# A second set of open pages, one signal a pass, and evenly spaced indirect transfers in a routed mixture of experts with a recurrence

## What is computed

```python
xn = layernorm(x)
# attention part: a recurrence over tokens, with a gate
xn2 = layernorm(xn) * ln_w + ln_b
u = xn2 @ Ws.T + bs + xn2 @ Wi.T + bi              # 16 numbers a token
h = tanh(h @ A.T + u_t)                            # one token after another
s = (H @ Wo.T + bo) * sigmoid(xn2 @ Wg.T + bg) + xn
# feed-forward part: 16 experts, 4 chosen for each token, and a shared one
scores = sigmoid(xn @ gate_w.T)
idx = top_k(scores + gate_b, 4)
w = scores[idx] / sum(scores[idx]) * 2.5
y = sum over the 4: w_k * (silu(xn @ w1_k.T) * (xn @ w3_k.T)) @ w2_k.T
y = y + shared expert(xn)
out = x + s * silu(y)
```

## Time and profile before

| what | value |
|---|---|
| median of 3 runs | 443.7 us (442.36 to 444.87) |
| profiled execution, first to last instruction | 513.9 us |
| mean granted TensorE clock | 0.837 of full |
| TensorE, DVE, ACT, POOL busy | 339.1, 311.1, 251.0, 265.4 us |
| DMA | 109.27 MB, mean 213 GB/s |

### The profile page before, as it was taken

The page is one execution under the profiler, slowest core; times in us unless marked ns, Lnnn a source line. Parts: engine busy times, 40 slices in busy tenths (PEclk is TensorE's granted clock), DMA queues, the critical chain, the costliest instruction groups (busy, mean ns, idle before and its releaser), DMA issues.

```text
span 513.9 us, 10001 instructions
## 1 busy us (share of the span) xinstructions
PE 339.1 (66%) x3107; PEld 261.7 (51%) x3107; DVE 311.1 (61%) x977; ACT 251.0 (49%) x462; POOL 265.4 (52%) x278
## 2 busy tenths in 40 slices
PE   0365566849467786976799968797876968645210
PEld 0352443626355665755698846575654756433100
DVE  4899776676703545545643626786776555346745
ACT  1851666536434455443787746565664644422000
POOL 2005377766646566655600165766555554436773
PEclk9976698797876889888999989999997898676555
DMA  7998499425443566654779768899977777436653
GB/s 247 305 328 281 129 343 331 161 86 201 143 165 127 175 186 201 196 172 156 216 220 269 227 192 268 281 282 285 285 243 211 249 217 225 128 119 194 174 160 126
DMA packets 88675, 109.27 MB, mean 213 GB/s; under 512 B 9649, under 2 KB 78002, under 8 KB 88626
## 3 DMA queue, kind: packets, MB, share of 16 engines
q1 hardware_dynamic: 74656, 74.47, 45.7%
q0 software_dynamic: 12288, 33.57, 20.7%
q10 hardware_dynamic: 1682, 0.59, 0.4%
HBM read 55.91 MB, written 52.69 MB: 211 GB/s over the span
## 4 chain that ended last, share of the span: by engine, by line
PE 35%; another core or an unknown queue 12%; issue 10%; ACT 8%; DVE 6%; POOL 5%; DMA 1%; ACTq 1%; POOLq 0%; DVEq 0%
PE bank L850 13%; PE bank L872 8%; PE bank L656 6%; POOL xn_parts L638 5%; PE bank L863 3%; ACT xn_f L1851 3%; PE bank L898 2%; ACT sh_h L1868 1%; ACT y_ring L1875 1%; ACT xn_f L1859 1%; ACT x_ring L1881 1%; PE bank L948 1%; DVE mix_sb L1371 1%; PE bank L774 1%
## 5 line engine op out<-in xcount | busy, mean ns | idle before, releaser
L638 POOL DMA_INDIRECT xn_parts<-y_slots,slot_u x128 | 127.2, 994 | 126.2 <-PE bank L656 39.6
L619 POOL DMA_INDIRECT x_slots<-xn_parts,slot_u x128 | 131.7, 1029 | 115.1 <-DVE slot_u L1253 36.0
L850 PE MATMUL bank<-w_all,xn_f 128*128 (+1 forms) x864 | 122.2, 295 | 22.2 <-issue 11.5
L850 PEld LDWEIGHTS bank<-w_all,xn_f 128*128 128x128 f16 x864 | 87.3, 106 | 44.8 <-issue 30.6
L1524 DVE SCALAR_TENSOR_TENSOR xn_f<-bank,xn_f 128x256 f32<-128x256 f32 x72 | 30.5, 424 | 111.9 <-ACT xn_f L1859 69.3
L1851 ACT ACTIVATE xn_f<-bank 128x1024 f16<-128x1024 f16 x72 | 73.5, 1022 | 36.7 <-remote 22.3
L872 PE MATMUL bank<-w_all,sh_silu 128*128 (+1 forms) x432 | 68.2, 299 | 5.5 <-ACT y_ring L1875 4.2
L1875 ACT ACTIVATE y_ring<-bank 128x512 f32<-128x512 f32 x72 | 42.9, 596 | 54.4 <-PE bank L872 33.7
L1859 ACT ACTIVATE xn_f<-bank 128x256 f32<-128x256 f32 x72 | 27.5, 382 | 55.0 <-remote 32.4
L656 PE MATMUL bank<-ident_h,w_stage 128*128 128x128 f16 x576 | 48.6, 231 | 1.5 <-issue 1.4
L872 PEld LDWEIGHTS bank<-w_all,sh_silu 128*128 128x128 f16 x432 | 41.8, 106 | 14.5 <-issue 7.5
(11 more groups left out here) (215 smaller groups left out, 456.9 us busy)
## 6 DMA issues: line engine op xcount, KB each, us to landing
w_stage<-x_slots SPq DMA_DIRECT2D x72, 256.0 KB
y_slots<-y_ring SPq DMA_DIRECT2D x72, 256.0 KB
x_slots<-zero_h SPq DMA_DIRECT2D x10, 1024.0 KB
x_ring<-in_x SPq DMA_DIRECT2D x32, 256.0 KB
w_stage<-in_w13t SPq DMA_DIRECT2D x17, 256.0 KB
x_ring<-in_x SPq DMA_DIRECT2D x8, 512.0 KB, 7.7
out<-mix_sb SPq DMA_DIRECT2D x15, 256.0 KB
w_stage<-in_w2t SPq DMA_DIRECT2D x17, 128.0 KB
```

The costliest lines, as they stand in the source:

```text
L619: eng.indirect_dma_start(out=x_slots, out_offset=bass.IndirectOffsetOnAxis(ap=slot_u[:, n * TOPK + k:n * TOPK + k + 1], axis=0), in_=xn_pa ...
L638: eng.indirect_dma_start(out=fin_y[:, r, j, k, :], out_offset=None, in_=y_slots[0:2 * READY_PAIR[c] * P, :], in_offset=bass.IndirectOffset ...
L850: mm = eng.matmul(gu[:, j * 2 * F:(j + 1) * 2 * F], xg_T[:, n % 2, ((j * 2 + px) * KD + k) * P:((j * 2 + px) * KD + k + 1) * P], weights_o ...
```

## The change

- **Pages.** The open pages 0 to 15 are closed after the first 12 tiles. The second set, pages 64 to 79, takes what is left of all later tiles. There are 160 pages in 80 pairs. Pairs 0 to 15 are full pages of the first 12 tiles, 16 to 23 the first open set, and both need those 12 tiles alone; 24 to 31 need 20 tiles; 32 to 79 need all scatters. `READY_PAIR` is 32 for units 0 to 5 as before, and 8 higher for the others (56, 64, 72, 80). The second group's page arithmetic on DVE is the first group's (`pages_full`, `room_open`); before, it had 23 small operations.
- **Signals.** TensorE gives one signal, `pair_pass`, with the last instruction of a pass; the four semaphores of the pair's steps and those of the recurrence and the mixing are gone. `pair_x` runs three ahead and `pair_y_down` three behind, so there are 83 passes.
- **Recurrence.** One step in each pass, in passes 1 to 27.
- **Transfers.** From scatter 61 on, and ahead of the gathers of units 0 to 11, POOL writes a 128-column tile (`space`) and waits for it, in place of `half_pair`. Units 0 to 9 stand at passes 40, 44, and on to 76; the mixing begins at pass 40 and not 31.

The diff, cut to its core:

```diff
-PAGES = MAIN_PAGES + EXPERTS
+PAGES = MAIN_PAGES + 2 * EXPERTS
...
-    OPEN_AT = KNOWN[1]
-    PAIRS = [*range(E, E + OPEN_AT, 2), *range(0, E, 2), *range(E + OPEN_AT, PAGES, 2)]
+    OPEN = [0, E + KNOWN[1]]
+    PAIRS = [*range(E, E + KNOWN[0], 2), *range(0, E, 2), *range(E + KNOWN[0], PAGES, 2)]
     NPAIR = len(PAIRS)
-    PHASE_PAIR = [0, KNOWN[0] // 2, KNOWN[1] // 2]
-    FILL_PIECES = [(first, first + 8) for first in range(E + KNOWN[1], PAGES, 8)]
-    FILLED_AHEAD = (0, 4, len(FILL_PIECES))
+    PHASE_PAIR = [0, (E + KNOWN[0]) // 2, (E + KNOWN[1]) // 2]
+    FILL_PIECES = [(first, first + 8) for first in range(OPEN[1], PAGES, 8)]
+    FILLED_AHEAD = (0, 6, len(FILL_PIECES))
...
-    READY_PAIR = [PHASE_PAIR[2] + EXPERTS // 2 if (c + 1) * 2 <= TILE0[1] else
-                  EXPERTS // 2 + CHOICES * max(TILE0[2], BT * -(-(c + 1) * 2 // BT)) // 2 for c in range(NT // 2)]
+    READY_PAIR = [PHASE_PAIR[2] if (c + 1) * 2 <= TILE0[1] else
+                  E + CHOICES * max(TILE0[2], BT * -(-(c + 1) * 2 // BT)) // 2 for c in range(NT // 2)]
...
-    XB_RING, YS_RING, AHEAD = 6, 5, 5
+    XB_RING, YS_RING, AHEAD = 6, 5, 6
+    X_AHEAD, H_BEHIND, DOWN_BEHIND = 3, 1, 3
+    PASSES_OF_PAIRS = NPAIR + DOWN_BEHIND
...
-    PER_HEAD_STEP, PER_HALF_SCATTER, PER_HALF_GATHER = 1.4, 1.65, 1.3
+    PER_HEAD_STEP, SPACER = 1.4, 128
     HEAD_FREE = 3
     HEAD_SCATTERS = HEAD_FREE + int(HEAD_FIRST[NB] * PER_HEAD_STEP)
-    SCATTER_HALF, GATHER_HALF = 5, 74
+    ROW_UNITS = 4
 
...
-        SCAN0 = [6, 24]
-        SHIFT = {21: 0, 48: 1}
+        SCAN_PASS = (1, 2 + WARM)
+        SHIFT_PASS = tuple(first + steps for first, steps in zip(SCAN_PASS, STEPS))
         OUT_SLOT = 43
-        CHECK, FALLBACK, PARTS = 50, 54, 55
-        UNIT_PAIR = tuple(40 + 10 * c // 3 for c in range(10))
-        STATES_SLOT = 86
+        CHECK, FLAG, FALLBACK, PARTS = 85, 87, 90, 91
+        UNIT_PAIR = tuple(40 + 4 * c for c in range(10))
...
-        MIX_SLOT = {93 + 6 * c: c for c in range(NU)}
+        MIX_SLOT = {120 + 6 * c: c for c in range(NU)}
...
+        def mix_pass(c):
+            return next(slot for slot, unit in MIX_SLOT.items() if unit == c) // SLOTS
+
+        def scan_place(n):
             for p in range(2):
-                at_ = slot - SCAN0[p]
-                if 0 <= at_ < STEPS[p] // 2 * 3 and at_ % 3 < 2:
-                    return p, at_ // 3 * 2 + at_ % 3
+                if 0 <= n - SCAN_PASS[p] < STEPS[p]:
+                    return p, n - SCAN_PASS[p]
             return None
 
         def unit_place(slot, offset):
...
+        def passed_after(n):
+
+            return n + 3
...
-                    eng.wait_ge(pair_t, n - XB_RING + 1)
+                    eng.wait_ge(pair_pass, passed_after(max(n - XB_RING - X_AHEAD, -2)))
...
-            def half_pair(h):
-
-                if h % 2:
-                    eng.wait_ge(pair_gu, h // 2 - 1)
-                else:
-                    eng.wait_ge(pair_t, h // 2)
+            def space(i):
+
+                eng.memset(spacer[:, :], 0.0).then_inc(spaced, 1)
+                eng.wait_ge(spaced, i + 1)
 
             def beside_scatter(i):
 
                 if HEAD_FREE <= i < HEAD_SCATTERS:
                     head_step(int((i - HEAD_FREE) / PER_HEAD_STEP))
                 elif i >= HEAD_SCATTERS:
-                    half_pair(SCATTER_HALF + int((i - HEAD_SCATTERS) / PER_HALF_SCATTER))
-
-            def beside_gather(i):
-
-                h = GATHER_HALF + int(i / PER_HALF_GATHER)
-                if h <= 2 * NPAIR:
-                    half_pair(h)
+                    space(i - HEAD_SCATTERS)
 
             def slot_x(s):
...
-                    beside_gather(c * FT * TOPK + i)
+                    if c < NU - ROW_UNITS:
+                        space(TOPK * NT - HEAD_SCATTERS + c * FT * TOPK + i)
...
+            eng.wait_ge(h_ones, 1)
...
             pair_x(0)
-            pair_x(1)
+            pair_x(1).then_inc(pair_pass, 1)
             eng.wait_ge(scored, NB)
             eng.wait_ge(u_scaled, 1)
             pair_up(0)
-            for n in range(NPAIR + 2):
-                if n + 2 < NPAIR:
-                    pair_x(n + 2)
+            pair_x(2).then_inc(pair_pass, 1)
+            for n in range(PASSES_OF_PAIRS):
                 beside(SLOTS * n)
                 if n + 1 < NPAIR:
-                    pair_up(n + 1)
+                    last = pair_up(n + 1)
                 beside(SLOTS * n + 1)
-                if 1 <= n <= NPAIR:
-                    pair_h(n - 1)
+                if n + X_AHEAD < NPAIR:
+                    last = pair_x(n + X_AHEAD)
+                if 0 <= n - H_BEHIND < NPAIR:
+                    last = pair_h(n - H_BEHIND)
                 beside(SLOTS * n + 2)
-                if n >= 2:
-                    pair_y_down(n - 2)
+                if (step := scan_place(n)) is not None and n > 1:
+                    last = scan_step(*step)
+                if n in SHIFT_PASS:
+                    scan_shift(SHIFT_PASS.index(n))
+                if n >= DOWN_BEHIND:
+                    last = pair_y_down(n - DOWN_BEHIND)
+                last.then_inc(pair_pass, 1)
             for c in range(len(UNIT_PAIR), NU):
                 shared_down(c)
...
+            def pages_full(phase):
+
+                base, end = (0, PAGE0[SECOND_GROUP])[phase], page_end[:, phase, :]
+                f, rows, open_at = new_pages[phase], full_rows[phase], open_row[phase]
+                eng.wait_ge(counted, phase + 1)
+                if phase:
+                    eng.wait_ge(page_step, base)
+                eng.tensor_scalar(count_i[:, :], count_cols(phase), 0.0, None, ALU.add).then_inc(page_step, 1)
...
+                eng.wait_ge(page_step, base + 3)
+                eng.tensor_tensor_scan(end, f[:, :], zero_e[:, :], page_end[:, 0, E - 1:E] if phase else float(E),
+                                       ALU.add, ALU.add).then_inc(page_step, 1)
...
+                    eng.tensor_scalar(beyond, at_, float(OPEN[1] * P), float(E * P), ALU.is_ge, ALU.mult).then_inc(slot_step, 1)
+                    eng.wait_ge(slot_step, base + 3)
+                    eng.scalar_tensor_tensor(out=beyond, in0=past, scalar=1.0, in1=beyond, op0=ALU.is_lt,
+                                             op1=ALU.mult).then_inc(slot_step, 1)
...
             pair_up(0)
-            for n in range(NPAIR + 2):
-                if (step := scan_place(SLOTS * n)) is not None:
+            pair_split(0)
+            for n in range(PASSES_OF_PAIRS):
+                beside(SLOTS * n)
+                if (step := scan_place(n)) is not None:
                     scan_sum(*step)
-                beside(SLOTS * n)
-                if (step := scan_place(SLOTS * n + 1)) is not None:
-                    scan_sum(*step)
+                if n in SHIFT_PASS:
+                    scan_shift(SHIFT_PASS.index(n))
+                if 0 <= n - H_BEHIND < NPAIR:
+                    pair_h(n - H_BEHIND)
                 if n + 1 < NPAIR:
                     pair_up(n + 1)
-                if n < NPAIR:
-                    pair_split(n)
+                    pair_split(n + 1)
                 beside(SLOTS * n + 1)
-                if 1 <= n <= NPAIR:
-                    pair_h(n - 1)
                 beside(SLOTS * n + 2)
...
             pair_up(0)
-            for n in range(NPAIR + 2):
-                if n + 2 < NPAIR:
-                    pair_x(n + 2)
+            pair_x(2)
+            pair_split(0)
+            for n in range(PASSES_OF_PAIRS):
                 beside(SLOTS * n)
+                if n >= DOWN_BEHIND:
+                    pair_y_out(n - DOWN_BEHIND)
                 if n + 1 < NPAIR:
                     pair_up(n + 1)
-                if n < NPAIR:
-                    pair_split(n)
-                beside(SLOTS * n + 1)
+                if (step := scan_place(n)) is not None:
+                    beside(SLOTS * n + 1)
+                    scan_step(*step)
+                if n + X_AHEAD < NPAIR:
+                    pair_x(n + X_AHEAD)
+                if n + 1 < NPAIR:
+                    pair_split(n + 1)
+                if scan_place(n) is None:
+                    beside(SLOTS * n + 1)
                 beside(SLOTS * n + 2)
-                if n >= 2:
-                    pair_y_out(n - 2)
             for c in range(len(UNIT_PAIR) - 1, NU - 1):
                 if in_tail(c, SILU):
                     silu(c)
```

253 lines of the change are left out of this document (98 added, 155 removed).

## The result

The change takes 495.9 us (median, 494.65 to 496.7), before 443.7: a ratio of 1.119, 95% interval 1.115 to 1.123. It is 52 us slower. The forecast was 455, in a range from 420 to 468: the direction was right, the size was short by 41 us.

What follows compares the result with a forecast made beforehand. With unexplained waits stripped, POOL was taken as nearly full in the gathers. Scatters end at 231.7, first gather 255.8, unit 6 at 333, units 6 to 11 to 407, then 48.9: sum 456. Forecast 455 us, range 420 to 468.

Steps and rivals of the forecast that it cites:

- spacing paid: The forecast's main case for the whole kernel: 1.50 to 1.60 us a transfer, time 455, range 446 to 466, chance 0.50.
- Stripping 70 us: Whole span: unexplained waits taken as the profile's cost and removed, 70.2 us from the span of 513.9 to median 443.7.
- A span near 476 beside a median near 456: Whole kernel: the changed kernel's profiled span would be near 476 us, the unstripped walk, against a stripped sum of 456.
- whether median and span keep their old ratio: Sign in the changed kernel's profile: if median and span kept their old ratio, the stripping was the wrong step.
- The head at zero: Head: less DVE page arithmetic and two more 1 MB fills together taken as zero, bounds -2.5 and +6 us.
- The spacer's price: POOL's transfers behind memsets: 1.55 us each, range 1.40 to 1.65; scatters' even spacing costs 14 us.
- Signals, the step that failed: TensorE's passes: no gain in 2.64 us passes; recurrence passes 3.7 us for the first 20, then 3.1; pass 29 at 236.
- passes bind: Rival, slower: if DVE's loop makes the first 27 passes 4.2 us or more, pass 29 at 250, time 470; chance 0.08.
- The second open set: Pages: pair 32 still waits for all scatters; first gather at 255.8, 3.8 us earlier than before; unit 6 needs pair 55.
- Spacing is nearly free: Rival, faster: transfers 1.33 to 1.42 us apart, under 1.46 deciding, passes bind; 432 to 440 us, chance 0.23.
- It gains where it says and pays it back: Rival, no change: at 1.46 to 1.48 us a transfer, the kernel takes 442 to 446 us; chance 0.09.
- The stalls are real: Rival, faster: unexplained waits are transfers crowding each other, so the whole shrinks alike to 411 us; chance 0.10.

Runs made afterwards that it cites:

- e16: The kernel before with the second open set and the spacer, keeping the old signals and two recurrence steps a pass: 459.6 us, 1.038 of before.
- e13: The kernel before with the second open set, old signals and order, one recurrence step a pass and mixing from pass 40: 1.010 of before.
- e5: The kernel before, unchanged, profiled on the chip that ran the whole change beside it: 443.1 us, span 442.8.
- e6: The whole change, run on the same chip as the kernel before: 1.121 of before.
- e9: The kernel before with the second open set alone, on a chip where before takes about 443 us: 1.008 of before.
- e15: The kernel before with the spacer alone, in place of half_pair: 1.068 of before.
- e17: The change with a second signal in each pass behind pair_up, and the silu and its product moved earlier: 492.2 us, 1.108 of before.
- e11: The change with the combining operations of units 0 to 9 on 16 columns of 256, leaving out work: 480.3 us, 1.082 of before.
- e12: The change with combining of units 0 to 9 and the mixing's two operations a unit cut to 16 columns: 472.8 us, 1.066 of before.
- e1: The kernel before with the second open set alone, on a slower chip where before takes 521.9 us: 1.077 of before.

## Why the prediction was wrong

It forecast "spacing paid", slower, and so it was; but the largest cost, the signals, was put at nearly nothing behind pair 31. e16 is the kernel of the sum with the old signals (and two recurrence steps a pass, which e13 shows to matter little), so the steps can be held against it and against the change.

| step | forecast (stripped) | pages, spacer (e16) | the change |
|---|---|---|---|
| end of the last scatter | 231.7 | 232.5 | 232.0 |
| TensorE goes on in pass 29 | 236 | 237.1 | 250.0 |
| y of pair 31 | 252 | 251.6 | 268.1 |
| first gather | 255.8 | 255.7 | 272.7 |
| unit 6 | 333 | 334.5 | 364.7 |
| unit 12 | 407 | 406.2 | 440.6 |
| end | 456 | 456.8 | 493.6 |

- **What bounds before.** Right: POOL nearly full in the gathers, the recurrence slow, TensorE at 2.64 between. Each is in e5's trace.
- **Stripping 70 us.** Right in amount, wrong in what it was. In e5 and e6 span and time agree within 2 us, so the profile costs nothing there, and the waits of the trace were most likely a slower chip's. In e5 the first gather is at 264.9 where I had 259.6, and the tail starts at 392.9 where I had 394.8. "A span near 476 beside a median near 456" was wrong: they are the same number, within 2 us. (By that trace's own 4.3 us a pair the unstripped walk would have unit 6 at 363, not 353.) The test that the prediction named, whether median and span keep their old ratio, spoke for the stripping, since the ratio went from 1.158 to 0.995; but it can't tell a cost of the profile from a slower chip.
- **The head at zero.** Right as a difference: scatter 60 starts at 131.1, in e5 at 132.2. But the stripping had put it at 126.2, 6 us too early, and scatter 61 at 127.8, where e16 has 133.6. A price of 1.55 a scatter instead of 1.48 made up for 4.7 of these 5.8 us. That e16 ends its scatters within 1 us of the forecast is in that part luck.
- **The spacer's price.** Right in kind and a little high: 1.55 forecast, 1.46 from start to start with nothing else in the way, 1.48 over the last 67 scatters of e16. It is 0.20 more than the 1.26 from one transfer to the next in e5, the least that its waits leave. The Trainium skill, Perfetto Trace Analysis, section GPSIMD Engine Instruction, says to time this engine start to start. Two memsets in a row are 0.14 apart, which was too little for a memset with a wait behind it; transfer to transfer, also start to start, gives the 0.20, and the memset's reported 0.22 was near it. The price decides only where POOL is the bound: 28.9 us on the kernel before, 2 to 3 on the kernel with the signals.
- **Signals, the step that failed.** There were two terms. *In the recurrence* I took the loop as 3.7 and then 3.1 us a pass, and put TensorE at pass 29 at 236. e13 has 3.38 and shows that number good for the old signals; with the change it is 4.70 over 17 pairs, TensorE reaches pass 29's check at 247.1 and goes on at 250.0, and y of pair 31 is 16.5 us later than in e16. My loop had the right operations in series, and 3.7 is not far from the 3.37 of the round shown. What it had wrong is the other work, which I spread evenly at 1.1 us a pair. It comes in lumps, TensorE's routing products stand behind it in the same pass, and VectorE and ACT then wait for the end of that pass: four passes of 7.9 to 9.8 us, with a lower granted clock behind TensorE's idle time. The rival "passes bind" had the recurrence right, at 0.08: its condition, 4.2 us or more, came true (4.22 over the 24 pairs whose y is copied in passes 4 to 27), and so did its 250 for pass 29. It took nothing for the passes behind, hence 470. *Behind pair 31* I took the pace of before over, 3.38 a pair with gathers, because "in the 2.64 us passes nothing waits". That holds for passes without other work and was wrongly carried to those with units and mixing: pairs 31 to 55 take 93.0 us in the change and 79.3 in e16, 13.7 more, and the time from unit 6 to the end 6.6 more. Together 36.8 us, the whole difference between the spans of e16 and the change. TensorE's idle time in 268 to 447 of the change is 36.5 us, in the same 48 pairs of e16 18.8; the mixing's product is 14.0 of the difference.
- **The tail.** 48.9 forecast, 50.6 in e16, 53.0 in the change.
- **The second open set.** Right: the start of the gathers gains (3.8 us forecast, 9.2 in e16 against e5, 15 in e9), and pair 55 takes it back. The wait for pair 24's block that it removes was 8.1 us of TensorE in e5.
- **The rivals.** "Spacing is nearly free" was to decide under 1.46 a transfer; it lay at 1.46 to 1.48, and e15 pays 28.9 us and e16 11.7 over e9, so it falls. "It gains where it says and pays it back" had just this price as its condition, 1.46 to 1.48, and 442 to 446 us as its time; even with the old signals it is 459.6 (e16). It had multiplied the price by all 163 transfers, but by the prediction's own sum unit 6 waits for pair 55 and pass 29 is held at 236 by the recurrence too, so that of the gathers only the 48 of units 6 to 11 count in full. "The stalls are real" falls for the chips at 443 us.

Which part of the order costs what behind pair 31 is open beyond this: e16 shows that the signals, with the order and the places that came with them, are the loss; e17 that the silu's place is about a third of it; e11 and e12 that the passes shrink when VectorE has less to do, but the same cut was not tried beside the old signals.

## What to carry to other kernels

Ask of a coarser signal not what is now idle, but which work must now fit between two signals one after another: write down the ring of operations over the engines in the order of their queues, with everything that stands between them, and compare its length with the pass. A stage that showed no wait tells nothing about a stage with more work in it. Write down the fullest pass too and not the mean one: here four of 17 passes held most of the recurrence's loss. And before a span is corrected, find a second trace of the same kernel: here 70 us between span and median were most likely another chip.

## What the runs showed of the hardware

The same kernel took 443 us on some chips and 521.9 on one, in 4 to 19 runs on each chip, all within 1% of their median. The fast passes are 2.64 us on both; what differs are releases without a record. e1 and e9 are one kernel on the two chips: e1's chain has 16% of them, and e9 has none, neither in its chain, which covers three quarters of the span, nor in the list of its waits. Chains by engine, e1 first:

```profile
PE 33%; issue 18%; another core or an unknown queue 16%; DVE 16%; ACT 10%; POOL 4%; DMA 2%; ACTq 1%; DVEq 0%; POOLq 0%; SPq 0%
...
PE 35%; DVE 16%; issue 9%; POOL 7%; DMA 3%; ACT 3%; ACTq 1%; POOLq 0%; DVEq 0%
```

What these waits are, no run tells. They change the worth of an edit: pages 1.077 there and 1.008 here, spacer 1.042 and 1.068, both together 1.114 and 1.038. A reading that fits, not tested by itself: with the passes slowed, pairs are dear and transfers cheap; where POOL is the bound, it is the other way round. TensorE's granted clock was 0.74 to 0.89 of full in the change's four long passes, in which TensorE was idle about half of the time; it was 1.00 in the short passes from 216 to 223, and also in the one of 5.1 us ahead of them, where TensorE was busy 3.05 us. A kernel tuned by traces of one of these chips may be tuned for the wrong bound on another.
